# Eight equal chunks in the first stage, the lead of the maxima spread over six of them, gate and up in two places

## What is computed

```python
xn = _layernorm(x, axis=-1)
q, kv = xn @ Wq, xn @ Wkv                  # split in 16 heads of 16
q, kv = rotary(q) * DH ** -0.5, rotary(kv)
attn = softmax(einsum('bmd,bnd->bmn', q, kv))
out = einsum('bij,bjd->bid', attn, kv)     # heads joined again
attention = out @ Wout + bout
gate, up = xn @ (w_gate / 127).T, xn @ (w_up / 127).T
ffn = (silu(gate) * up) @ (w_down / 127).T # hidden size 768
result = x + attention + ffn
```

## Time and profile before

| what | before |
|---|---|
| median of 3 runs | 914.42 us (913.4 to 915.58) |
| profiled execution | 918.31 us, its span 916.4 us |
| PE busy | 847.3 us, 92% |
| DVE, ACT, POOL busy | 763.9, 695.1, 187.2 us |
| mean granted TensorE clock | 0.986 |

### The profile page before, as it was taken

One profiled execution on the slowest core, in us unless ns is written; L12 is line 12 of the kernel. 1 busy time (PEld: TensorE's weight loads), 2 busy tenths in 40 slices (PEclk: granted clock), 3 DMA queues, 4 the chain that ended last, 5 costly groups with the idle time before them and its releaser, 6 DMA issues.

```text
span 916.4 us, 18500 instructions
## 1 busy us (share of the span) xinstructions
PE 847.3 (92%) x7018; PEld 319.0 (35%) x7018; DVE 763.9 (83%) x932; ACT 695.1 (76%) x1317; POOL 187.2 (20%) x411
## 2 busy tenths in 40 slices
PE   2999999999799999999999999999999999999798
PEld 1455565564322222222222223222222222222234
DVE  5787776698989999999999999988999998999502
ACT  4354655523389999999998999898989999998583
POOL 4333444433300010000111111111211111121020
PEclk9999999999989999999999999999999999999799
DMA  9012111011001111111111122111111221111222
GB/s 328 18 47 73 55 47 46 31 64 46 19 19 30 27 26 26 39 30 32 37 43 49 44 59 55 49 43 42 43 49 51 57 53 46 43 44 48 65 69 78
DMA packets 58494, 47.39 MB, mean 52 GB/s; under 512 B 18189, under 2 KB 48717, under 8 KB 58405
## 3 DMA queue, kind: packets, MB, share of 16 engines
q1 hardware_dynamic: 58404, 46.20, 17.8%
HBM read 28.57 MB, written 16.90 MB: 50 GB/s over the span
## 4 chain that ended last, share of the span: by engine, by line
PE 64%; DVE 17%; ACT 10%; issue 5%; DMA 2%; SPq 1%; POOL 0%; DVEq 0%; ACTq 0%
PE ps L677 22%; PE ps L694 11%; PE ps L660 11%; DVE negmax L1147 10%; ACT arena L946 7%; PE ps L574 6%; PE ps L536 4%; PE ps L603 4%; PE ps L702 3%; DMA arena<-inv_d 1%; DVE side L1053 1%; DVE stats L1005 1%; PE ps L589 1%; DMA x_all<-x_dram 1%; DVE arena L1040 1%
## 5 line engine op out<-in xcount | busy, mean ns | idle before, releaser
L1147 DVE TENSOR_REDUCE negmax<-ps 128x2 f32<-128x1024 f32 x512 | 594.3, 1216 | 53.5 <-PE ps L694 53.2
L946 ACT ACTIVATE arena<-ps 128x512 f32<-128x512 f32 x1024 | 555.8, 597 | 61.2 <-PE ps L660 39.9
L677 PE MATMUL ps<-arena 128*32 128x256 f32 (+1 forms) x3664 | 317.7, 419 | 0.3 <-ACT arena L946 0.2
L660 PE MATMUL ps<-qs,ks 51*128 51x512 f16 x1024 | 200.2, 386 | 24.3 <-ACT arena L946 23.4
L694 PE MATMUL ps<-ks,qs 48*128 48x512 f16 x1024 | 200.0, 388 | 7.8 <-DVE negmax L1147 7.7
L694 PEld LDWEIGHTS ps<-ks,qs 48*128 48x128 f16 x1024 | 49.1, 93 | 184.3 <-issue 147.6
L677 PEld LDWEIGHTS ps<-arena 128*32 128x32 f32 x3664 | 72.6, 108 | 115.4 <-issue 101.9
L660 PEld LDWEIGHTS ps<-qs,ks 51*128 51x128 f16 x1024 | 50.9, 93 | 138.7 <-ACT arena L946 109.1
L574 PE MATMUL ps<-arena,side 128*128 128x512 f16 x384 | 88.1, 384 | 6.8 <-DVE side L1053 5.9
L1281 POOL TENSOR_TENSOR side<-side 128x512 f16<-128x512 f32 x48 | 55.8, 1165 | 75.8 <-ACT side L880 75.8
L874 ACT ACTIVATE side<-ps 128x512 f32<-128x512 f32 x48 | 28.5, 593 | 55.9 <-PE ps L574 55.9
(11 more groups left out here) (78 smaller groups left out, 456.3 us busy)
## 6 DMA issues: line engine op xcount, KB each, us to landing
parts_d<-arena SPq DMA_DIRECT2D x64, 128.0 KB
x_all<-x_dram SPq DMA_DIRECT2D x8, 512.0 KB, 8.0
qs<-parts_d SPq DMA_DIRECT2D x64, 64.0 KB, 1.9
ks<-parts_d SPq DMA_DIRECT2D x64, 64.0 KB, 1.9
o_d<-arena SPq DMA_DIRECT2D x124, 32.0 KB
arena<-o_d SPq DMA_DIRECT2D x24, 128.0 KB
arena<-inv_d SPq DMA_DIRECT2D x48, 64.0 KB
out_dram<-arena SPq DMA_DIRECT2D x24, 128.0 KB, 1.8
```

Of the source, the lines that this page charges most:

```text
L660: mm = pe.matmul(ps[:, score_bank(ls, 2 * half + a), :], ks[ring][top:top + ROWS, kt * P:(kt + 1) * P], qs[ring][top:top + ROWS, half * CH ...
L677: mm = pe.matmul(ps[32 * j:32 * j + 32, 7, cols], vstage[pl % 2][:, j % 2, kt, :], probs[PER_STEP * (kt % PBUF) + j][:, cols], start=(kt = ...
L946: act.activation(probs[PER_STEP * (kt % PBUF) + j], ps[:, score_bank(ls, j), :], ACT.Exp).then_inc(exp_done, 1)
L1147: dve.tensor_reduce(negmax[pl % 2][:, h, :, kt], ps[:, 2 * h:2 * h + 2, :], AX.X, ALU.max, negate=True).then_inc(max_done, 1)
```

## The change

- **Chunks.** All eight have one form: PLAIN and the hand-written order of chunks 6 and 7 go. In chunks 2 to 7 each of the last four `gate_up` has one unit of the lead ahead of it (UNITS = 4), and DVE has that unit's maximum ahead of the product. All units of the lead use banks 2 and 3 and wait for the maximum before (`max_done, n`).
- **Places.** `gate_up` uses banks 6, 7 and 0, 1 in turn; `turn_x` comes after the second `gate_up`; `low_x` comes after the last product and `inverse`; `copy_x` is split in two, and ACT does `silu(c, j)` ahead of `high(c, j - 1)`.
- **Start.** `copy_x(0)` comes ahead of ACT's wait for the ratio.
- **Hand-over.** `turn_qk(7)` comes after all `gate_up`; `down(7)` is split in `down_most` and `down_rest` with the transpose of the first pair's maxima between them; `split_max(0, 0)` comes ahead of POOL's work of chunk 7.
- **The end.** `load_last(0)` is moved into slot `PAIRS - 2`, behind its `load_tile`.

```diff
-PLAIN = NCHUNK - 2
-GATE_BANKS = (6, 0, 2, 6, 0, 2)
-GATE_BANKS_6 = (0, 2, 0, 2, 4, 6)
-GATE_BANKS_7 = (4, 4, 6, 4, 6, 4)
+GATE_BANKS = (6, 0)
+LEAD_BANK = 2
+LEAD_FROM = CPB
+UNITS = 2 * LEAD // (NCHUNK - LEAD_FROM)
...
@@ sync
             def slot(p, j, load, rows, tiles):
...
                     load_tile(b, t, k)
+                if p == PAIRS - 2:
+                    sp.wait_ge(inv_stored[0], 16 * QH * (PAIRS - RING) // 2)
+                    load_last(0, front_in)
                 if load:
...
-            for k in range(2):
-                sp.wait_ge(inv_stored[k], 16 * QH * (PAIRS - RING) // 2)
-            load_last(0, front_in)
@@ tensor: project, gate_up, turn_qk
+                    if c and t == 0:
+                        pe.wait_ge(silu_done, KH * c)
+                        pe.wait_ge(hid_done, KH * c)
+                    if t == 2 and c > LEAD_FROM:
+                        pe.wait_ge(max_done, UNITS * (c - LEAD_FROM))
...
+                elif j == 1:
+                    pe.wait_ge(rope_read, CT * c + 2)
                 else:
...
+                    pe.wait_ge(silu_done, KH * c + j - 1)
+                    pe.wait_ge(hid_done, KH * c + j - 1)
...
+                    if g == 2:
+                        pe.wait_ge(silu_done, KH * c + 5)
+                        pe.wait_ge(hid_done, KH * c + 5)
@@ tensor: new
+            def down_most(c, t):
+
+                if t == 0:
+                    pe.wait_ge(hh_done, KH * (c + 1) - 1)
+                    pe.wait_ge(hl_done, KH * (c + 1) - 1)
+                pe.wait_ge(lo_done, 4 * c + t + 1)
+                for n in range(2 * (KH - 1)):
...
+            def lead(n):
+
+                pl, kt, h = n // MAXES, n % MAXES // 2, n % 2
+                if n % MAXES == 0:
+                    pe.wait_ge(stacks_in[pl], 16 * 8)
+                pe.wait_ge(max_done, n)
+                for a in range(2):
+                    top = HEAD_ROWS * a
+                    mm = pe.matmul(ps[:, LEAD_BANK + a, :], qs[pl][top:top + PROD, kt * P:(kt + 1) * P],
+                                   ks[pl][top:top + PROD, h * CHUNK:(h + 1) * CHUNK], start=True, stop=True)
+                mm.then_inc(max_scores, 1)
...
+            for c in range(NCHUNK):
                 project(c)
...
+                gate_up(c, 0)
+                gate_up(c, 1)
+                if c + 1 < NCHUNK:
+                    turn_x(c + 1)
+                units = lead_units(c)
+                for j in range(2, KH):
+                    if units:
+                        if j == 2:
+                            pe.wait_ge(rope_read, CT * (c + 1))
+                        lead(units[j - 2])
                     gate_up(c, j)
                 turn_qk(c)
...
+            last = NCHUNK - 1
+            for t in range(2):
+                down_most(last, t)
+            pe.wait_ge(identh_ready, 1)
+            turn_max(0, 0, (max_done, 2 * LEAD), LEAD_BANK)
+            for t in range(2, CT):
+                down_most(last, t)
+            for t in range(CT):
+                down_rest(last, t)
@@ scalar
             roots(CT, 2 * CT)
+            for k in range(KD):
+                copy_x(0, k)
             act.wait_ge(ratio_done, 1)
...
                 high(c, 0)
+                if more:
+                    copy_x(c + 1, 0)
+                high(c, 1)
                 silu(c, 2)
...
+                if more:
+                    copy_x(c + 1, 1)
                 for j in range(3, KH):
+                    silu(c, j)
                     high(c, j - 1)
-                    silu(c, j)
                 high(c, KH - 1)
...
+            high_qk(NCHUNK - 1)
@@ vector
+                gated(c, 0)
+                gated(c, 1)
+                units = lead_units(c)
+                for j in range(2, KH):
+                    if units:
+                        n = units[j - 2]
+                        maxima(0, n // 2, n % 2, LEAD_BANK)
                     gated(c, j)
                 if c < 3:
                     inverse(c + 2, 2 * CT * (c + 1), 2 * CT * (c + 2))
+                if c + 1 < NCHUNK:
+                    low_x(c + 1)
```

More of the change, by code:

```diff
@@ L436, in _, with load_last @@
             load_mrows(0, 0)
+            def load_last(g, landed):
+                rows = P if g == 0 else BACK_ROWS
+                for k in range(CPB):
+                    tok = slice(k * CHUNK, (k + 1) * CHUNK)
+                    sp.dma_start(olast[k][0:rows, g, :], o_d[BATCH - 1, g, 0:rows, tok]).then_inc(landed, 16)
+                    src = inv_groups[BATCH - 1, g, 0:rows // DH, tok]
+                    sp.dma_start(ilast[k][0:rows, g, :], src.unsqueeze(1).to_broadcast((rows // DH, DH, CHUNK))
+                                 ).then_inc(landed, 16)
             def slot(p, j, load, rows, tiles):
@@ L892, in _ @@
             roots(CT, 2 * CT)
+            for k in range(KD):
+                copy_x(0, k)
             act.wait_ge(ratio_done, 1)
             act.activation(scale[:, 0:1], ratio[:, 1:2], ACT.Sqrt, scale=4.0).then_inc(root_done, 1)
-            copy_x(0)
-            for c in range(PLAIN):
+            for c in range(NCHUNK):
+                more = c + 1 < NCHUNK
                 if c:
                     high_qk(c - 1)
-                normalise(c + 1)
+                if more:
+                    normalise(c + 1)
                 silu(c, 0)
@@ L968, in rows @@
                 n = MPARTS * MAXES
-                act.activation(mrows[slot % 2][:, :], ps[0:n, turn_bank, 0:P // 2].bitcast(FP16), ACT.Copy
+                act.activation(mrows[slot % 2][:, :], ps[0:n, bank, 0:P // 2].bitcast(FP16), ACT.Copy
                                ).then_inc(mrows_done, 1)
@@ L1074, in rope_chunk @@
                         rotated(c, t - 1)
-                    if c == NCHUNK - 1 and t == 2:
-                        gated(PLAIN, 0)
                 rotated(c, CT - 1)
@@ L1121, in _ @@
                     moments(2 * CT * (c + 1), 2 * CT)
-                for j in range(3):
-                    gated(c, j)
-                low_x(c + 1)
-                for j in range(3, KH):
+                gated(c, 0)
[5 more added lines that the diff above has]
+                        maxima(0, n // 2, n % 2, LEAD_BANK)
                     gated(c, j)
@@ L1337, in split_max, with stage_values @@
                 pool.tensor_tensor(mp[:, :, 2, :], mrest[:, :, :], mwhole[:, :, :], ALU.subtract).then_inc(msplit_done, 1)
-            split_max(0, 0)
+            for c in range(NCHUNK):
+                add_bias(c)
+                if c + 1 == NCHUNK:
+                    split_max(0, 0)
+                keep_values(c)
+                for j in range(KH):
+                    low_hid(c, j)
+            def stage_values(p, batch, slot, pair):
+                for a in range(2):
+                    src = v_all[:, bass.ds(batch * BT, BT), bass.ds(pair * 2 * DH + a * DH, DH)]
+                    ins = pool.tensor_copy(vstage[slot % 2][:, a, :, 0:DH], src)
+                ins.then_inc(v_staged, 1)
             pool.wait_ge(y_done, CT * NCHUNK)
```

335 lines of the change are left out of this document (82 added, 253 removed).

## The result

The changed kernel takes **908.26 us** (median of 4 runs, 906.57 to 909.42) against 915.0 (913.4 to 916.9) of the kernel before on the same chip, 6.7 us less. The recorded ratio, which is not that of the two medians, is 0.9918 (95% interval 0.9898 to 0.9938), or 7.5 us. 905.9 was forecast, with 900 to 912 as the range. A second set of 7 runs, on another chip, gives 908.17 and 0.9945 (0.9922 to 0.9967): 6.3 us by the medians, 5.0 by the ratio. The profiled execution took 906.57 (span 904.8, clock 0.989), that of before 918.31.

What follows compares the result with a forecast made beforehand. PE, busy 847 of 916 us, was taken as the bound. First scores 0.6 us later and 9.1 us saved at the end give -8.5: profiled 909.8, median 905.9 us after a 3.9 us offset; range 900 to 912.

Steps and rivals of the forecast that it cites:

- The tail: Near the end, moving load_last(0) removes PE's 6.1 us wait for a tile and 2.9 us of slow clock: 9.1 us.
- the rival of the late tile: At the end, load_last(0)'s transfers slow the tile from behind; two thirds of the gain lost, 912 to 914; chance 0.09.
- Start: Before chunk 0, earlier copy_x(0) lets the rotations start at 21.6 instead of 22.6 without a 1.4 wait: 2.5 us gained.
- the low value: The start's 2.5 us gain, assuming DVE's cast of wg waits for POOL's; without that, 1.4 us better.
- So the cadence stays 27.95: Chunks 0 to 2: DVE's chain from one gated(c,0) to the next stays 27.95 us; chunks 0 and 1 cost nothing.
- The order of ACT: Chunks 0 to 2: silu(j) ahead of high(j-1) shortens end of gated(0) to end of gated(5) from 9.15 to 7.9 us.
- the term of `low_x`: Chunks 0 to 2: low_x(c+1), added in front of low_qk on DVE's chain, takes 1.3 us.
- Clock: Chunks 0 to 2: two half-clock stretches behind the waits for gated, 3.5 us; bounds are none and three.
- every wait costs the clock: Three half-clock stretches in chunks 0 to 2 and 3.5 us more at the loop's start: 5 us more, 911; chance 0.14.
- Chunks 3 to 7: PE stays the bound, with five periods of 26.81 us less one turn_x: 133.2 us, ending turn_qk(7) at 233.4.
- Hand-over: From the end of turn_qk(7), through chunk 7's stores and load_mrows, to the first scores: 12.4 us.
- Loop start: Start of the attention loop: cold clock in both kernels, taken as even (-1 to +1.5 us).

Runs made afterwards that it cites:

- the copies put back: Changed kernel with copy_x(0) again behind ACT's wait for the ratio, as in the kernel before: 910.55 us, ratio 0.9961, 2.4 us more than the changed kernel.
- the tail undone: Changed kernel with load_last(0) again ahead of slot 30, between the loop and that slot: 917.21 us, ratio 1.0032 to the kernel before.
- The fillers: Changed kernel plus 12 unread matmuls in PE's queue ahead of the wait for gated in each of chunks 0 to 2: 905.14 us, ratio 0.9895.
- the tail alone: Kernel before with one edit, load_last(0) moved into slot 30 behind its load_tile: 905.43 us, ratio 0.9914, 9.0 us less than before.
- the best version: Changed kernel with moments behind gated(c,1), chunk 7's q and k transposes early, and load_mrows(0,0) ahead of SP's wait for stores: 897.55 us, ratio 0.9827.
- 3.3 us of statistics: Changed kernel with DVE's moments of chunks 0 to 2 behind gated(c,1) instead of ahead of gated(c,0): 900.91 us, ratio 0.9847.

## Why the prediction was right or wrong

**The tail: right, and more than all of the gain.** -9.1 forecast, -9.0 measured alone (-7.9 by the ratio), 9.0 lost when undone. Nothing became late in its place, and the four broad transfers behind the tile didn't delay it: POOL divides 3.9 us after the first transfer for `inv_d` goes out, so the rival of the late tile is out.

**Start: the number came out by luck.** -2.5 forecast, 2.4 by the copies put back. But DVE did not let its cast wait for POOL's: it ran ahead of it, at 16.79, and POOL's came at 17.73. The rotations start at 17.66, where I had 21.6. The first wait ends at 30.04, 29.75 and 31.24 in three executions with the early copies (the last is of the kernel with the tail undone) and at 35.17 with the copies late. That is some 5 us, outside my bounds of 1 and 3.9, and the slower chunks behind it take part of it back. That the low value stood on the port lock was a wrong reason.

**"So the cadence stays 27.95": wrong by 0.6 a chunk.** At full clock it is 28.54, 1.2 us in the two. The order of ACT did what I laid out: with late copies `gated(0, 0)` begins at 34.33 and the last product ends at 43.02, 8.0 after the end of the first, 7.9 forecast. What failed is the term of `low_x`, put at 1.3 us: from its start to `low_qk` it is 1.73 (46.23 to 47.96). It now runs while POOL adds the bias, and DVE (L1004) and POOL (L1212) both take longer, 1.81 for 1.29 and 3.75 for 2.77 us. In the changed kernel:

```profile
42.78 1.81 DVE L1004 TENSOR_TENSOR arena<-arena 128x512 f16<-128x512 f32 x2
...
41.43 3.75 POOL L1212 TENSOR_TENSOR x_all<-x_all,bias 128x256 f32<-128x256 f32 x4
```

In chunks 3 to 7, where PE is the bound and it costs nothing, the same work stands beside POOL's `low_hid` and takes 2.94:

```profile
126.72 2.94 DVE L1004 TENSOR_TENSOR arena<-arena 128x512 f16<-128x512 f32 x2
126.39 2.73 POOL L1200 TENSOR_TENSOR side<-side 128x512 f16<-128x512 f32 x2 [1.00 <-ACT side L854]
```

The Trainium skill, "SBUF — State Buffer", section "Who interferes with whom", has a DVE instruction with two inputs in SBUF contend with what POOL reads there; the rows agree with that. I had used the rule at the start, where it changed nothing, and not here.

**Clock: the count about right, the price on the wrong side.** I took two half-clock stretches in chunks 0 to 2 and saw two in one profile of the changed kernel and three, the last of them a short one, in the other. I charged both kernels alike for theirs. But in the kernel before a stretch behind the first or second wait costs nothing, since DVE is paced by ACT there (its products waited 1.18 each) and the next wait takes it up; only one behind the third wait costs, 1.3 us (8.61 to `project(3)` for 7.28). Its profile happened to hold one there. In the changed kernel a stretch behind the first or the second costs 1.7 and one behind the third 1.1 (11.53 from there to `project(3)`, 10.43 where the clock stayed up). The fillers give this term its size: 3.0 us, about as much as the whole first stage costs more (2.8), where I had forecast +0.6 for it. Of the rival "every wait costs the clock" the direction was right, its size too large: neither did every wait cost it nor did the loop lose 3.5.

**Chunks 3 to 7: right.** Period 26.81 forecast; `project` starts at 127.60, 154.41, 181.21 and 208.03 in the changed kernel (26.81, 26.80, 26.82), the one ahead of them 27.25. **Hand-over: right**, 11.9 us after `turn_qk` for 12.4. **Loop start: +0.6 for "even"**: from the first scores to `project_tile` it is 605.65 us (605.06 in the tail alone). The first scores run at half clock now, 0.61 us for 0.39.

**The two sums.** By medians 914.4 - 9.0 + 2.8 = 908.2 was measured and 914.4 - 9.1 + 0.6 = 905.9 forecast: the error lies in the first stage, and inside it terms that were too small and too large stood against each other. For a profiled execution I had 909.8, and 906.57 and 908.12 came; for the median I had 905.9, and 908.2 came. The two are off in opposite directions because I took 3.9 us, by which one profiled execution of before lay above the median, to hold for the changed kernel. There it was -1.7 and -0.1. The profile of the tail alone, which has the same first stage, shows where 2.4 of the 3.9 lie: it has `project(3)` at 98.27 for 100.63, its start 1.1 earlier and its third stretch at full clock (and it still lies 1.4 above its own median). From the first scores to the end of the span eleven of the twelve profiles with the moved tail agree within 1.5 us (657.8 to 659.3; the best version's, an execution 3.4 above its median, has 660.7), so most of an execution's distance from its median lies in the first stage, in the start and in the clock. The profiles alone would make the first stage of the changed kernel even or a little faster; the timed runs make it 2.8 slower. How the clock falls in the runs that were not profiled can't be seen, and how these 2.8 us divide over its terms stays open by about as much.

## What to carry to other kernels

A wait that the engine before it absorbs hides the clock's falls as well; before a change takes the slack out of a chain, ask what else the slack was paying for, and move work off the chain first (here 3.3 us of statistics, worth 7). Short critical loads go ahead of long ones that nobody needs yet in the same queue: that one move was worth 9 us, more than the whole change gained. And one profile against another can show the wrong sign for a change of 0.3%; time one part alone, and the other undone.

## What the runs showed of the hardware

- The same program falls to half clock in different places in different executions: behind the first and third wait in one, behind all three in another. Behind a wait of 2.85 the 32 matmuls took 7.07 or 8.75; with 12 fillers in each wait it was 7.07 both times.
- Two 128x512 subtractions on DVE and four 128x256 additions on POOL that overlap in time both take longer than alone (1.81 for 1.29, 3.75 for 2.77 us); beside two of POOL's 128x512 subtractions those on DVE take 2.94.
